# Two chained matrix products on one core: narrower plain block and wider product blocks, block sums in PSUM, shared weight slots, a first weight load in two pieces

## The chip, the cores and the metric

The kernel runs on one core of one Trainium2 chip. The metric is the device time of one execution in microseconds; less is better. The runs shown are the median of three executions of the kernel before.

## The reference

`x` has 8 batch elements of 256 rows and 1024 columns. For each element an adapter matrix (1024 x 1024, picked by an id) is applied, and a layer with low-rank experts is applied to the result. Everything is float32.

```
y    = x[b] @ weight[ids[b]].T                     # 256 x 1024
base = y @ base_W.T + base_b                       # 1024 outputs
p    = softmax(y @ router_W.T + router_b)          # 15 logits
w    = per expert (8): sum of the 8 largest p that map to it
h    = y @ A.T                                     # 8 experts x 16 ranks = 128 columns
out  = x + base + ((h * w) @ B) * 2
```

## The kernel before, in words

**Splits.** Almost every float32 operand is split into a high part in the type fp32r (a copy on ACT) and a low part (original minus high part, on DVE). A product is then high times high, plus high times low, plus low times high: three matmuls in fp32r. In stage 1 the moving operand carries high and low part of x side by side, so there the three are one of 512 and one of 256 columns.

**Work per element.** The eight elements run one after the other; element 0 and element 1 are written out, elements 2 to 6 are a loop, element 7 is written out again. An element has two stages on TensorE (PE).

- Stage 1 makes y transposed, in 8 chunks of 128 outputs. A chunk is `stage1_chunk`: 8 pairs of a 512-column matmul (L783) and a 256-column one (L785), into one of two PSUM banks `y_ps`. Before a chunk, PE waits for the chunk's weight split (`w_lo`) and for the running sum `y_sum` of the chunk two before it, which frees its bank. The first two chunks of element 0 skip the split and run as plain float32 matmuls (`stage1_float32`, L796; each shows as two records), which wait for `w0_in` and `x0_in`.
- Stage 2 multiplies y by the base matrix. `plain` (L807 to L809) does A, the router and the first NP = 288 base columns in one pass of 128 + 16 + 288 = 432 columns, 48 matmuls an element. The other 736 base columns are two halves N1 and N2 of NH = 368. With the two halves of the contraction and the two row tiles of y this is a 2 x 2 by 2 x 2 block product; it is done with 7 block products (`product`, L819 to L821, 12 matmuls each) in place of 8, on sums of blocks: S1, S2, S3 of y blocks and T1 to T4 of base blocks. Element 0 uses the plain 8 products, since the sums of base blocks are not there yet. `transposes` (L839) turns the gated h; `lora_b` (L833 to L835) multiplies it by B, into the same PSUM banks.

**Around PE.** Per chunk, ACT copies one half of the bank out and casts weights (`w_hi`, L362) and y (`y_hi`, L358); DVE adds the other half (`y_sum`, L503), and makes `w_lo` (L485) and `y_lo` (L507). After each pair of chunks DVE makes the y block sums (L513, L514, L516, `sums`) in SBUF, ACT casts them (`sums_hi`) and DVE makes `s_lo` (L520). S4 needs y and S2 and comes from `fourth`. DVE also does the router's softmax and top-8 on small tiles, adds the bias to the residual tile `res` and adds each finished PSUM bank into `res`. In element 1 DVE makes T3 and T4 (L679, L682) between chunks, and the low parts of T1 to T4 (L686, L690, L695) behind the last chunk.

**Order.** Each engine's order is written out by hand in its block, and semaphores tie the engines. Weights have 4 slots: SP loads the chunk for slot c when PE has finished the chunk that used it, ACT and DVE split it three chunks ahead. SP's queue carries all loads but the first two halves of x (ACT's queue), and all stores but those of element 0 (POOL's queue). Chunks 4 to 7 of element 0 are loaded early, into memory that later holds other tiles (`early_raw`).

```python
def stage1_chunk(b, c):
    s = c % W_SLOTS
    pe.wait_ge(w_lo_done, split(b, c))
    pe.wait_ge(y_sum_done, OC * b + c - 1)
```

## Time and profile before

| | |
|---|---|
| median of 3 runs | 406.89 us (406.59 to 407.56) |
| the profiled execution | 407.73 us, its span 405.9 us |
| granted TensorE clock, mean | 1.00 of 2.4 GHz |
| PE busy (matmuls) | 98% of the span |
| weight loads (PEld) busy | 92% |
| DVE busy | 73% |
| ACT busy | 38% |
| DMA | 64.7 MB, mean 159 GB/s |

The span runs from the first to the last instruction; the execution's own time is 1.8 us more. PE is one row of matmuls and PEld one row of the loads of their stationary operand, which overlap the matmuls. The recorded length of a matmul holds its way through the array, so matmuls overlap in the records; what one costs in a dense stretch is the time from its start to the next one's start.

### The profile page before, as it was taken

To read this page: it belongs to the slowest core of one execution; us is meant where nothing else is said; L and a number is where in the kernel's file an instruction comes from. 1 tells how busy PE (TensorE), PEld (TensorE's weight loads), DVE (VectorE), ACT (ScalarE), POOL (GpSimd) and SP (SyncE) were. 2 spreads that over 40 slices of the span, in tenths; PEclk is the share of its full clock that TensorE was granted. 3 is DMA by queue.
4 is the path that set the end of the run, shared out by engine and by line. 5 is a ranking of instruction groups with operands and counts; after the bars stand their busy time and mean duration, and the time that the engine had idled before them with its cause. 6 is when DMAs were issued, how large, how long until landed. Compare 5 with 4: busy or idle time off the path is not lost.

```text
span 405.9 us, 6358 instructions
## 1 busy us (share of the span) xinstructions
PE 398.8 (98%) x2278; PEld 371.6 (92%) x2278; DVE 295.8 (73%) x575; ACT 154.9 (38%) x236; POOL 2.0 (0%) x10
## 2 busy tenths in 40 slices
PE   7999999899999999999999999999999999999997
PEld 7889998789988999889998899989998899988996
DVE  2778985999959973788638885499754997467743
ACT  3675425563046220562216630165203643045200
POOL 0000000000000000000000000000000000000000
DMA  8999016660067602585025830468105770154002
GB/s 299 399 400 393 20 42 216 256 214 0 2 242 278 204 0 96 174 297 157 0 111 199 303 110 0 157 218 291 57 7 200 245 272 0 52 200 164 1 2 103
DMA packets 24878, 64.73 MB, mean 159 GB/s; under 512 B 2466, under 2 KB 11042, under 8 KB 24866
## 3 DMA queue, kind: packets, MB, share of 16 engines
q1 hardware_dynamic: 24290, 62.48, 42.9%
q10 hardware_dynamic: 288, 1.05, 0.8%
q0 software_dynamic: 288, 1.05, 0.6%
q8 instruction: 7, 0.11, 0.1%
q14 instruction: 5, 0.04, 0.0%
HBM read 56.18 MB, written 8.39 MB: 159 GB/s over the span
## 4 chain that ended last, share of the span: by engine, by line
PE 91%; DVE 4%; DMA 2%; ACT 1%; issue 1%; SPq 0%
PE y_ps L783 26%; PE y_ps L785 13%; PE pl_ps L807 6%; PE pl_ps L809 6%; PE pl_ps L808 6%; PE x_ps L821 5%; PE x_ps L820 5%; PE x_ps L819 5%; PE z_ps L819 3%; PE z_ps L820 3%; PE z_ps L821 3%; DMA w_raw<-in_wT 2%; PE y_ps L796 2%; PE w_ps L819 1%; PE w_ps L821 1%; PE w_ps L820 1%
## 5 line engine op out<-in xcount | busy, mean ns | idle before, releaser
L783 PE MATMUL y_ps<-x_split,w_hi 128*128 128x512 f32 x496 | 172.9, 394 | 1.2 <-DVE y_sum L503 1.2
L785 PE MATMUL y_ps<-x_split,w_lo 128*128 128x256 f32 x496 | 137.6, 277 | 0.0
L783 PEld LDWEIGHTS y_ps<-x_split,w_hi 128*128 128x128 f32 x496 | 93.0, 187 | 22.9 <-DVE w_lo L485 0.9
L785 PEld LDWEIGHTS y_ps<-x_split,w_lo 128*128 128x128 f32 x496 | 93.2, 188 | 0.0
L485 DVE TENSOR_TENSOR w_lo<-w_raw,w_hi 128x1024 fp32r<-128x1024 f32 x58 | 70.8, 1224 | 12.6 <-ACT w_hi L362 10.3
L354 ACT COPY y_sum<-y_ps 128x256 f32<-128x256 f32 x62 | 23.1, 373 | 122.2 <-PE y_ps L785 122.2
L362 ACT CAST w_hi<-w_raw 128x1024 fp32r<-128x1024 f32 x58 | 60.7, 1050 | 10.3 <-DMA w_raw<-in_wT 10.1
L503 DVE TENSOR_TENSOR y_sum<-y_ps,y_sum 128x256 f32<-128x256 f32 x62 | 26.1, 421 | 29.8 <-ACT y_sum L354 29.5
L807 PE MATMUL pl_ps<-pl_hi,y_hi 128*128 128x432 f32 x128 | 45.7, 357 | 0.2 <-DVE y_lo L507 0.2
L809 PE MATMUL pl_ps<-pl_hi,y_lo 128*128 128x432 f32 x128 | 45.8, 358 | 0.0
L808 PE MATMUL pl_ps<-pl_lo,y_hi 128*128 128x432 f32 x128 | 45.7, 357 | 0.0
L591 DVE TENSOR_TENSOR res<-x_ps,res 128x368 f32<-128x368 f32 x29 | 15.7, 540 | 30.0 <-PE x_ps L821 17.9
L358 ACT CAST y_hi<-y_sum 128x512 fp32r<-128x512 f32 x32 | 19.9, 621 | 21.1 <-DVE y_sum L503 20.6
L507 DVE TENSOR_TENSOR y_lo<-y_sum,y_hi 128x512 fp32r<-128x512 f32 x32 | 22.2, 692 | 5.5 <-ACT y_hi L358 2.7
L807 PEld LDWEIGHTS pl_ps<-pl_hi,y_hi 128*128 128x128 f32 x128 | 24.0, 188 | 1.8 <-DVE y_lo L507 0.6
L808 PEld LDWEIGHTS pl_ps<-pl_lo,y_hi 128*128 128x128 f32 x128 | 24.0, 187 | 1.0
L809 PEld LDWEIGHTS pl_ps<-pl_hi,y_lo 128*128 128x128 f32 x128 | 24.0, 188 | 0.9
L821 PE MATMUL x_ps<-st_hi,y_lo 128*128 128x368 f32 x64 | 21.1, 329 | 0.0
L819 PE MATMUL x_ps<-st_hi,y_hi 128*128 128x368 f32 x64 | 21.1, 329 | 0.0
L820 PE MATMUL x_ps<-st_lo,y_hi 128*128 128x368 f32 x64 | 21.0, 329 | 0.0
L588 DVE TENSOR_TENSOR res<-res,bias 128x1024 f32<-128x1024 f32 x16 | 18.8, 1218 | 0.0
L820 PE MATMUL x_ps<-st_lo,s_hi 128*128 128x368 f32 x56 | 18.5, 330 | 0.0
(140 smaller groups left out, 600.3 us busy)
## 6 DMA issues: line engine op xcount, KB each, us to landing
w_raw<-in_wT SPq DMA_DIRECT2D x60, 512.0 KB, 3.3
res<-in_x SPq DMA_DIRECT2D x16, 512.0 KB, 4.6
x_raw<-in_xT SPq DMA_DIRECT2D x14, 512.0 KB, 5.9
out<-res SPq DMA_DIRECT2D x13, 512.0 KB, 2.6
early_raw<-in_wT SPq DMA_DIRECT2D x4, 512.0 KB, 8.7
hi_raw<-in_base_t SPq DMA_DIRECT2D x4, 368.0 KB, 9.9
st_raw<-in_base_t SPq DMA_DIRECT2D x4, 368.0 KB, 10.1
pl_raw<-in_base_t SPq DMA_DIRECT2D x2, 576.0 KB, 12.1
```

What stands on the lines that cost most here:

```text
L354: nc.scalar.copy(y_sum[:, ORDER[c], :], y_ps[:, c % 2, T:2 * T]).then_inc(y_part_done, 1)
L362: nc.scalar.copy(w_hi[:, c % W_SLOTS, :, :], w_raw[:, c % W_SLOTS, :, :]).then_inc(w_hi_done, 1)
L485: nc.vector.tensor_tensor(w_lo[:, s, :, :], w_raw[:, s, :, :], w_hi[:, s, :, :], ALU.subtract).then_inc(w_lo_done, 1)
L503: nc.vector.tensor_tensor(y_sum[:, o, :], y_ps[:, c % 2, 0:T], y_sum[:, o, :], ALU.add).then_inc(y_sum_done, 1)
L783: nc.tensor.matmul(y_ps[:, c % 2, :], w_hi[:, s, k, :], x_split[:, k, :, :].rearrange("p s t -> p (s t)"), start=(k == 0), stop=False)
L785: mm = nc.tensor.matmul(y_ps[:, c % 2, 0:T], w_lo[:, s, k, :], x_split[:, k, 0, :], start=False, stop=(k == KC - 1))
L807: nc.tensor.matmul(dst, hi, pl_hi[:, k, :], start=(c == 0), stop=False)
L808: nc.tensor.matmul(dst, hi, pl_lo[:, k, :], start=False, stop=False)
L809: mm = nc.tensor.matmul(dst, lo, pl_hi[:, k, :], start=False, stop=(c == KC - 1))
L819: nc.tensor.matmul(dst, hi(j), st_hi[:, j, block_of, :], start=begins and j == 0, stop=False, skip_group_check=not begins)
L820: nc.tensor.matmul(dst, hi(j), st_lo[:, j, block_of, :], start=False, stop=False, skip_group_check=not begins)
L821: mm = nc.tensor.matmul(dst, lo(j), st_hi[:, j, block_of, :], start=False, stop=(j == KH - 1), skip_group_check=not begins)
```

## The change

NP goes from 288 to 32, and so NH from 368 to 496, the `plain` pass from 432 to 176 columns. The memory for the wider blocks comes from the y sums: DVE writes S1, S2, S3 into the three PSUM banks `z_ps`, `w_ps`, `v_ps` (now one tensor `s_ps`), and their splits `s_hi`, `s_lo` lie over weight slots 2 and 3. So the sums are split once an element, behind the last chunk (`sums_hi`, `sums_lo` of 1536 elements), and chunks 2 and 3 of the next element are loaded only when `w_ps_done` says that the last product from the sums is through. Weights are split two chunks ahead, and that split now stands in front of the running sum of the chunk. `add_bias` is in two parts, one before the last running sums and one behind them; `add_plain` is one addition for both tiles. `plain` does most of its contraction for both row tiles first and the last pair of chunks at the end. The block splits are one instruction for each block (1984 elements). In element 0 the order of products is new: B00 for both tiles first, each added into a part of `res` that the same bank is then used for again (`p1_done`, `p1_added`), then B10, T1, B11. In element 1 the T sums and splits are spread over the chunks and stage 2. The first weight chunk comes in two loads of 256 KB, each with a semaphore.

```diff
-    NP = 288
+    NP = 32
...
+        s_hi = sb("s_hi", [P, 3, KH, P], F32R, over=at_w + 2 * 4 * KC * P)
+        s_lo = sb("s_lo", [P, 3, KH, P], F32R, over=at_w + (W_SLOTS + 2) * 4 * KC * P)
...
+        s_ps = bank("s_ps", [P, 3, 512])
+        z_ps, w_ps, v_ps = (s_ps[:, i, :] for i in range(3))
...
             def element(b, last=False):
...
-                    if c + W_SLOTS < OC or not last:
+                    if c + W_SLOTS < OC or (not last and c < W_SLOTS + 2):
                         sp.wait_ge(y_ps_done, OC * b + c + 1)
                         load_w(this if c + W_SLOTS < OC else nxt, (c + W_SLOTS) % OC)
...
                 if not last:
+                    sp.wait_ge(y_ps_done, OC * b + OC)
                     load_x(b + 1)
+                    sp.wait_ge(w_ps_done, b + 1)
+                    for c in (2, 3):
+                        load_w(nxt, c)
...
-            sp.dma_start(w_raw[:, 0, :, :], wT[bass.ds(id0, 1), 0].rearrange("a p k o -> (a p) k o")).then_inc(w0_in, 16)
+            for j in range(PIECES):
+                k = slice(j * KP, (j + 1) * KP)
+                sp.dma_start(w_raw[:, 0, k, :], wT[bass.ds(id0, 1), 0, :, k, :].rearrange("a p k o -> (a p) k o")).then_inc(w0_in[j], 16)
...
-            def sums_lo(b, j):
-                dve.wait_ge(s_hi_done, KH * (b - 1) + j + 1)
-                nc.vector.tensor_tensor(s_lo[:, j, :, :], s_raw[:, j, :, :], s_hi[:, j, :, :], ALU.subtract).then_inc(s_lo_done, 1)
+            def sums_lo(b):
+                dve.wait_ge(s_hi_done, b)
+                nc.vector.tensor_tensor(s_lo[:, :, :, :], s_ps[:, :, :].rearrange("p s (j t) -> p s j t", t=P), s_hi[:, :, :, :],
+                                        ALU.subtract).then_inc(s_lo_done, 1)
...
                 for c in range(OC):
+                    if not last or c + 2 < OC:
+                        adapter_lo(b, c + 2)
                     make_y_sum(b, c)
                     if c % 2:
                         sums(b, c // 2)
                         dve.wait_ge(s_done, KH * (b - 1) + c // 2 + 1)
                         make_y_lo(b, c // 2)
-                    if not last or c + 3 < OC:
-                        adapter_lo(b, c + 3)
-                    if c % 2:
-                        sums_lo(b, c // 2)
...
+            block_lo(1, B00, r00)
+            block_sum_1()
+            block_lo(2, B10, r10)
             masks()
-            block_sums_1_2()
             routing_logits(0)
+            dve.wait_ge(res_in[0], 16)
+            dve.wait_ge(p1_done, 1)
+            add(0, N2, w_ps[:, 0:NH]).then_inc(p1_added, 1)
+            t1_lo()
+            dve.wait_ge(res_in[1], 16)
+            dve.wait_ge(p1_done, 2)
+            add(1, N2, x_ps[:, 0:NH]).then_inc(p1_added, 1)
             routing_gates(0)
...
-            def plain(b, t, first=False):
-                dst = pl_ps[:, t, 0:PL]
-                for c, k in enumerate(PLAIN_ORDER):
...
+            def plain(b, first=False):
+                for t, part in ((1, 0), (0, 0), (1, 1), (0, 1)):
+                    for k in PLAIN_ORDER[:KC - 2] if part == 0 else PLAIN_ORDER[KC - 2:]:
...
-                product(z_ps, y_block(0, 0), T1, wait_blocks=1)
-                product(z_ps, y_block(1, 0), B11, begins=False, wait_blocks=2)
-                product(x_ps, y_block(0, 1), T1)
-                product(x_ps, y_block(1, 1), B11, begins=False).then_inc(b01_free, 1)
...
+                product(w_ps, y_block(0, 0), B00).then_inc(p1_done, 1)
+                product(x_ps, y_block(0, 1), B00).then_inc(p1_done, 1)
+                pe.wait_ge(blocks_lo_done, 2)
+                pe.wait_ge(p1_added, 1)
+                product(w_ps, y_block(1, 0), B10, begins=False)
+                pe.wait_ge(p1_added, 2)
+                product(x_ps, y_block(1, 1), B10, begins=False)
+                pe.wait_ge(t_lo_done, 1)
+                product(z_ps, y_block(0, 0), T1)
```

The first place where the order moves is DVE's in stage 2 of element 0, on which PE's new waits rest. `st_lo` and `st_raw`, `hi_raw` are the low parts and the raw blocks of the base matrix, `res<-s_ps` is the addition of the first B00 product. Before:

```order
L507 TENSOR_TENSOR y_lo<-y_sum,y_hi 128x2x256
L656 TENSOR_TENSOR st_lo<-hi_raw,st_hi 128x2x2x368
L653 TENSOR_TENSOR st_lo<-st_raw,st_hi 128x2x736
L656 TENSOR_TENSOR st_lo<-hi_raw,st_hi 128x2x2x368
L653 TENSOR_TENSOR st_lo<-st_raw,st_hi 128x2x736
L661 CAST map_f<-map_i 128x15
L664 TENSOR_SCALAR expert_mask<-map_f 128x15 x8
L672 TENSOR_TENSOR hi_raw<-hi_raw 128x4x368
L674 TENSOR_TENSOR st_raw<-st_raw,hi_raw 128x4x368
L540 TENSOR_TENSOR logits<-pl_ps,router_bias 128x30
```

And now:

```order
L515 TENSOR_TENSOR y_lo<-y_sum,y_hi 128x2x256
L668 TENSOR_TENSOR st_lo<-hi_raw,st_hi 128x4x496
L684 TENSOR_TENSOR hi_raw<-hi_raw 128x4x496
L668 TENSOR_TENSOR st_lo<-st_raw,st_hi 128x4x496
L672 CAST map_f<-map_i 128x15
L675 TENSOR_SCALAR expert_mask<-map_f 128x15 x8
L550 TENSOR_TENSOR logits<-pl_ps,router_bias 128x30
```

followed, behind the rest of the logits' work, by

```order
L600 TENSOR_TENSOR res<-s_ps,res 128x496
L702 TENSOR_TENSOR st_lo<-hi_raw,st_hi 128x4x496
L600 TENSOR_TENSOR res<-x_ps,res 128x496
```

The two additions of half-finished output (L600) are new; they stand behind three instructions on 1984 elements, the masks and the logits.

The second place is DVE's order in element 1, chunks 1 and 2, where PE waited before. Before:

```order
L503 TENSOR_TENSOR y_sum<-y_ps,y_sum 128x256
L513 TENSOR_TENSOR s_raw<-y_sum 128x128
L514 TENSOR_TENSOR s_raw<-y_sum 128x128
L516 TENSOR_TENSOR s_raw<-s_raw,y_sum 128x128
L507 TENSOR_TENSOR y_lo<-y_sum,y_hi 128x2x256
L485 TENSOR_TENSOR w_lo<-w_raw,w_hi 128x1024
L520 TENSOR_TENSOR s_lo<-s_raw,s_hi 128x384
L503 TENSOR_TENSOR y_sum<-y_ps,y_sum 128x256
L485 TENSOR_TENSOR w_lo<-w_raw,w_hi 128x1024
L679 TENSOR_TENSOR st_raw<-st_raw,hi_raw 128x4x368
L503 TENSOR_TENSOR y_sum<-y_ps,y_sum 128x256
```

And now:

```order
L493 TENSOR_TENSOR w_lo<-w_raw,w_hi 128x1024
L511 TENSOR_TENSOR y_sum<-y_ps,y_sum 128x256
L522 TENSOR_TENSOR s_ps<-y_sum 128x128
L523 TENSOR_TENSOR s_ps<-y_sum 128x128
L525 TENSOR_TENSOR s_ps<-s_ps,y_sum 128x128
L515 TENSOR_TENSOR y_lo<-y_sum,y_hi 128x2x256
L493 TENSOR_TENSOR w_lo<-w_raw,w_hi 128x1024
L511 TENSOR_TENSOR y_sum<-y_ps,y_sum 128x256
```

The split of the sums is gone from between the chunks, the weight split stands in front of the running sum, and the T sum that stood in front of chunk 3's running sum (L679) has moved to chunk 0.

## Rows read from the trace of the kernel before

**Rows 1.** The page, busy time of each engine and its share.

```profile
PE 398.8 (98%) x2278; PEld 371.6 (92%) x2278; DVE 295.8 (73%) x575; ACT 154.9 (38%) x236; POOL 2.0 (0%) x10
```

**Rows 2.** By stretch: its length, busy PE, PEld, DVE, ACT, POOL, then granted clock, DMA.

```profile
133.22:142.60 9.38, 9.38 (x51) 9.01 (x49) 8.14 (x14) 2.98 (x5) 0.00 (x0) 1.00 0.56 171
142.60:159.67 17.07, 17.07 (x106) 17.04 (x104) 10.34 (x30) 2.49 (x4) 0.00 (x0) 1.00 0.08 31
65.16:83.58 18.42, 17.21 (x98) 14.60 (x97) 16.03 (x29) 10.89 (x18) 0.00 (x0) 1.00 0.64 232
83.58:111.03 27.45, 26.95 (x154) 25.93 (x153) 25.90 (x47) 9.46 (x11) 0.00 (x0) 1.00 0.18 59
```

**Rows 3.** Timeline, the first matmuls of element 3's stage 1.

```profile
159.67 0.40 PE L783 MATMUL y_ps<-x_split,w_hi 128*128 128x512 f32 x1
159.90 0.28 PE L785 MATMUL y_ps<-x_split,w_lo 128*128 128x256 f32 x1
160.02 0.39 PE L783 MATMUL y_ps<-x_split,w_hi 128*128 128x512 f32 x1
```

**Rows 4.** Timeline, PE behind a wait in element 1's `plain`.

```profile
87.43 0.19 PEld L807 LDWEIGHTS pl_ps<-pl_hi,y_hi 128*128 128x128 f32 x1 [0.55 <-DVE y_lo L507]
...
87.54 0.19 PEld L808 LDWEIGHTS pl_ps<-pl_lo,y_hi 128*128 128x128 f32 x1
...
87.74 0.36 PE L808 MATMUL pl_ps<-pl_lo,y_hi 128*128 128x432 f32 x1
```

**Rows 5.** Timeline of element 2's stage 2: start, length, engine, line.

```profile
142.60 0.33 PE L819 MATMUL x_ps<-st_hi,y_hi 128*128 128x368 f32 x1
...
144.60 0.33 PE L819 MATMUL z_ps<-st_hi,s_hi 128*128 128x368 f32 x1
...
156.38 0.29 PE L833 MATMUL pl_ps<-b_hi,hwt_hi 128*128 128x288 f32 x1
156.51 0.29 PE L834 MATMUL pl_ps<-b_lo,hwt_hi 128*128 128x288 f32 x1
```

**Rows 6.** Timeline, weight loads behind the two 128-column transposes, element 1.

```profile
99.57 0.19 PEld L819 LDWEIGHTS w_ps<-st_hi,y_hi 128*128 128x128 f32 x1
...
99.68 0.19 PEld L820 LDWEIGHTS w_ps<-st_lo,y_hi 128*128 128x128 f32 x1
```

**Rows 7.** Timeline of DVE in element 0's stage 2.

```profile
33.44 1.68 DVE L656 TENSOR_TENSOR st_lo<-hi_raw,st_hi 128x1472 fp32r<-128x1472 f32 x1
35.04 1.69 DVE L653 TENSOR_TENSOR st_lo<-st_raw,st_hi 128x1472 fp32r<-128x1472 f32 x1
...
39.85 0.17 DVE L661 CAST map_f<-map_i 128x15 f32<-128x15 int32 x1
...
40.78 1.69 DVE L672 TENSOR_TENSOR hi_raw<-hi_raw 128x1472 f32<-128x1472 f32 x1
...
44.12 0.18 DVE L540 TENSOR_TENSOR logits<-pl_ps,router_bias 128x30 f32<-128x30 f32 x1
...
45.20 0.18 DVE L556 TENSOR_REDUCE row_sum<-prob 128x2 f32<-128x30 f32 x1
```

**Rows 8.** Timeline of PE, the first matmul behind element 0's stage 1.

```profile
31.11 0.36 PE L807 MATMUL pl_ps<-pl_hi,y_hi 128*128 128x432 f32 x1
```

**Rows 9.** DMA issues: count, KB each, median us from issue to landing.

```profile
w_raw<-in_wT SPq DMA_DIRECT2D x60, 512.0 KB, 3.3
```

**Rows 10.** Timeline, the change from float32 chunks to split chunks in element 0.

```profile
11.35 1.04 ACT L362 CAST w_hi<-w_raw 128x1024 fp32r<-128x1024 f32 x1 [0.23 <-DMA w_raw<-in_wT]
...
13.57 0.42 DVE L733 COPY y_sum<-y_ps 128x256 f32<-128x256 f32 x1
...
14.47 0.19 PEld L785 LDWEIGHTS y_ps<-x_split,w_lo 128*128 128x128 f32 x1
```

**Rows 11.** Timeline, the end of the program.

```profile
403.00 0.54 DVE L591 TENSOR_TENSOR res<-x_ps,res 128x368 f32<-128x368 f32 x1 [2.02 <-PE x_ps L835]
```

**Rows 12.** The tile `w_raw` to 40 us: count, shortest, median, longest ns, first and last start.

```profile
L796 PE MATMUL y_ps<-x_raw,w_raw x32: 379/379/483, 7.5 to 14.2; 128*128 128x256 f32 x32
```

More of the change, by code:

```diff
@@ L109, in adaln_ffn_kernel @@
         res = sb("res", [P, NT, D])
-        early_raw = [sb(f"early_raw{i}", [P, KC, P], over=at) for i, at in
-                     enumerate((at_s + 4 * KC * T, at_bias, at_res, at_res + 4 * D))]
+        x0_raw = sb("x0_raw", [P, KC, T], over=at_res)
+        early_raw = [sb(f"early_raw{i}", [P, KC, P], over=at_st + i * 4 * 7 * NH) for i in range(OC - W_SLOTS)]
         at_hwt = spot[0]
@@ L157, in adaln_ffn_kernel @@
         pl_in = [sem(f"pl_in{h}") for h in range(2)]
-        st_in = [sem(f"st_in{j}") for j in range(KH)]
+        upper_in = sem("upper_in")
+        lower_in = sem("lower_in")
         b_in = sem("b_in")
@@ L323, in _ @@
             for j in range(KH):
-                load_blocks(j)
+                load_upper(j)
+            for j in range(KH):
+                load_lower(j)
             for src, dst in ((expert_map, map_i), (router_b, router_bias)):
@@ L458, in _ @@
                 if c == 6:
-                    blocks_hi(0, 0)
-            blocks_hi(0, 1)
-            blocks_hi(1, 0)
-            blocks_hi(1, 1)
+                    act.wait_ge(upper_in, 16 * KH)
+                    act.wait_ge(w_lo_done, split(0, OC - 1))
+                    block_hi(B00, hi_raw[:, :, T4, :])
+            act.wait_ge(lower_in, 16 * KH)
+            block_hi(B10, st_raw[:, :, T4, :])
+            act.wait_ge(t_done, 1)
+            nc.scalar.copy(st_hi[:, :, T1, :], hi_raw[:, :, T2, :]).then_inc(t1_hi_done, 1)
+            block_hi(B11, st_raw[:, :, T3, :])
             exponential(0)
-            make_x_hi(1)
             act.wait_ge(b_in, 16)
@@ L609, in stage2 @@
                 add(1, N2, z_ps[:, 0:NH]).then_inc(z_added, 1)
+                if second:
+                    t3_lo()
+                else:
+                    fourth(b)
                 dve.wait_ge(x_ps_done, x_adds(b, 2))
@@ L614, in stage2 @@
                     fourth(b)
-                    fourth_lo(b)
-                if not last:
+                fourth_lo(b)
+                if not last and not second:
                     make_x_lo(b + 1)
@@ L621, in stage2 @@
                 if second:
+                    t4_lo()
+                    make_x_lo(b + 1)
                     dve.wait_ge(x_added, x_adds(b, 3))
-                    add_bias(b)
+                    for t in range(NT):
+                        add_bias(b, t)
                     dve.wait_ge(res_biased, 2 * b + 2)
@@ L703, in element @@
                         make_y_lo(b, c // 2)
-                    if not last or c + 3 < OC:
-                        adapter_lo(b, c + 3)
-                    if c % 2:
-                        sums_lo(b, c // 2)
-                    if isinstance(b, int) and b == 1 and c == 2:
-                        block_sum_3()
-                    if isinstance(b, int) and b == 1 and c == 6:
-                        block_sum_4()
-                if isinstance(b, int) and b == 1:
-                    t1_lo()
-                    t34_lo()
-                    t2_lo()
-                    routing_logits(b)
-                else:
-                    add_bias(b)
-                    fourth(b)
-                    fourth_lo(b)
-                    routing_logits(b)
+                    if second and c == 0:
+                        block_sum_4()
+                    if second and c == 4:
+                        t2_lo()
+                    if not second and c == 6:
+                        add_bias(b, 0)
+                if second:
+                    block_sum_3()
+                else:
+                    add_bias(b, 1)
+                sums_lo(b)
+                routing_logits(b)
                 stage2(b, last)
@@ L852, in first_stage2 @@
+                product(x_ps, y_block(0, 1), B00).then_inc(p1_done, 1)
[6 more added lines that the diff above has]
+                product(z_ps, y_block(0, 0), T1)
                 pe.wait_ge(hw_done, 1)
                 transposes()
-                product(w_ps, y_block(0, 0), B00)
@@ L855, in first_stage2 @@
-                product(w_ps, y_block(1, 0), B10, begins=False)
+                pe.wait_ge(blocks_lo_done, 3)
+                product(z_ps, y_block(1, 0), B11, begins=False)
                 pe.wait_ge(b_lo_done, 1)
                 pe.wait_ge(hwt_lo_done, 1)
+                lora_b(0, w_ps[:, 0:NH], N1).then_inc(w_ps_done, 1)
                 lora_b(0, z_ps[:, 0:NH], N2).then_inc(z_ps_done, 1)
-                lora_b(1, x_ps[:, 0:NH], N2).then_inc(x_ps_done, 1)
-                lora_b(0, w_ps[:, 0:NH], N1).then_inc(w_ps_done, 1)
+                lora_b(1, x_ps[:, 0:NH], N1).then_inc(x_ps_done, 1)
@@ L861, in first_stage2 @@
                 for t in range(NT):
                     lora_b(t, pl_ps[:, t, AR:PL], PLAIN).then_inc(pl_ps_done, 1)
-                product(v_ps, y_block(0, 1), B00)
-                product(v_ps, y_block(1, 1), B10, begins=False)
-                lora_b(1, v_ps[:, 0:NH], N1).then_inc(v_ps_done, 1)
+                product(v_ps, y_block(0, 1), T1)
+                product(v_ps, y_block(1, 1), B11, begins=False)
+                lora_b(1, v_ps[:, 0:NH], N2).then_inc(v_ps_done, 1)
             def stage2(b):
-                pe.wait_ge(pl_added, 2 * b)
```

211 lines of the change are left out of this document (102 added, 109 removed).

## Prediction, made blind

> **What bounds the kernel now.** The page comes first: matmuls are busy for 98% of the span, weight loads for 92%, DVE for 73% [rows 1]. PE is the bound, so I price PE's rows from start to start, and ask only where PE waits. In element 2 nothing waits: the busy time of both stretches equals their length, 9.38 us for `plain` and 17.07 us for the rest [rows 2]. The granted clock there is 1.00, the 2.4 GHz level. Element 1 is the exception. Its stage 2 takes 27.45 us against 9.38 + 17.07 = 26.45 us in element 2, and its chunks 2 to 7 take 18.42 us where six chunks of eight pairs at 0.347 us are 16.64 us [rows 2, 3]. That is 2.8 us of waiting on DVE; one of the waits, 0.55 us for `y_lo`, is shown [rows 4].
>
> What a matmul costs, start to start: 432 columns 9.38 / 48 = 0.195 us [rows 2]; 368 columns 2.00 / 12 = 0.167 us [rows 5]; 512 columns 0.23 and 256 columns 0.12 us [rows 3]; 288 columns 0.13 us [rows 5]. All lie on one line, columns / 2.4 GHz + 13 ns, within 2 ns. So 496 columns cost 0.220 us, between two known widths.
>
> **The narrow pass** is the term that decides, and no row shows a moving operand under 256 columns in fp32r. The line gives (176 + 32) / 2.4 = 0.087 us. But each matmul needs a weight load of its own, and the load for the next one starts when the present one starts. Behind a wait, where PE is empty, the first load starts at 87.43 and the second, which can begin once the first matmul streams, at 87.54; the second matmul starts at 87.74, one 0.195 us matmul later [rows 4]. Behind the transposes two loads are again 0.11 us apart [rows 6]. So a load takes 0.109 us before its matmul can stream. At 256 columns and more it is hidden (0.12 us); at 176 it is not. The bounds are 0.087 us (load hidden) and 0.120 us (the narrowest fp32r row, 256 columns). I take 0.109, the row that shows the load alone. The six 32-column matmuls of `lora_b` cost 0.109 each too, against 0.13 before.
>
> On this the Trainium skill, "TensorE: Matmul & The Clock Gate", section "Back-to-back issue gap", says columns / 2.4 + 2.5 ns for an isolated stream, with a floor near 25 ns. That is an estimate of 76 ns for 176 columns and would put the total near 396 us; the traced widths contradict its constant (13 ns, not 2.5). The same page's section "LDWEIGHTS (loading the stationary operand)" gives 128 / 1.2 = 107 ns for the load, which the 0.109 us row agrees with.
>
> **The change, part by part.**
> 1. *Elements 1 to 7, each.* `plain` 48 x (0.109 - 0.195) = -4.13 us. Seven products 84 x (0.220 - 0.167) = +4.45. `lora_b` on N1 and N2 12 x 0.053 = +0.64; its plain columns 6 x (0.109 - 0.132) = -0.14. Sum +0.82, times seven +5.7 us.
> 2. *Element 0* has eight products: -4.13 + 96 x 0.053 + 0.64 - 0.14 = +1.5 us.
> 3. *New waits in element 0.* PE reaches the second use of `w_ps` after `plain` 5.2 and two B00 products 5.3, 10.5 us behind stage 1. It waits there for DVE's first partial addition. DVE is done with `y_lo` at 33.44, 2.3 us behind stage 1, which ends at 31.11 [rows 7, 8]. A 1472-element instruction holds it 1.60 us (33.44 to 35.04), 1.09 ns an element, so 1984 take 2.15. Three of them, the masks 0.93 (39.85 to 40.78), the logits 1.08 (44.12 to 45.20) [rows 7], and an addition of 496 (0.5) end at 11.3. With the 0.2 us that PE takes behind a DVE result (DVE 13.57 + 0.42, seen below) that is a stall of 1.0 us; the second addition, behind one more 2.15 us split, costs 0.1. **+1.1 us.** T1's split, the gates and B11's split are 2 us or more ahead of PE.
> 4. *Element 1.* Out of each pair of chunks goes the split of the sums (0.5 us), and a 1.7 us T sum no longer stands in front of chunk 3's running sum. By the same lengths, laid out in DVE's new order, every running sum is 0.5 to 1 us early but that of chunk 5, level with PE. In stage 2 the 5.35 us of T3 and T4 splits lie in front of nothing PE needs. Of 2.8 us I leave 0.4: **-2.4 us.** If this is not so, what is late is `w_lo` of chunk 7, at one DVE instruction, 2 us.
> 5. *Sums split at once.* From the end of stage 1: y sum, y cast and `y_lo` 2.3, bias 1.1, then 1536 elements 1.7 us: 5.1 us. PE needs them after `plain` and one product, at 5.2 + 2.6 = 7.8. Hidden by 2.7 us; with a 0.087 us pass by 1.7. `fourth` (three instructions of 512 elements, 1.7 us) now stands in front of the second x addition, which needs the S2 product's end at 13.2 in any case; DVE has it by 14.0, PE asks behind the transposes and one more product, at 16.1. Nothing.
> 6. *Weight slots 2 and 3.* Their loads start 5.3 us before the element's end (two `lora_b` blocks of 0.66, the narrow one, the T4 product and its `lora_b`); a load lands in 3.3 us at the median [rows 9], a cast and a split of 1024 take 1.04 [rows 10] and 1.1. Chunk 2 needs them 5.5 us into the next element: 5 us to spare. Behind the waiting SP stand only the stores, which need later results. Without that cover, each late load would stop DVE's running sum too, since the split now stands in front of it. Nothing.
> 7. *First weight chunk in two loads.* PE starts at 7.45 us, waiting for it; half of it lands perhaps 0.9 us sooner. But PE then meets the next wait: chunk 2 of element 0 needs `y_sum` of chunk 0, which DVE does behind two weight splits that hang on the fourth weight load (landed at 11.35): it ends at 13.99, and PE's first split chunk streams from 14.47 [rows 10]. With 0.2 us behind DVE it can stream from 14.2. **-0.25 us** (between 0 and -0.3). The extra issue on SP delays nothing that PE waits for. The last addition and store are 128 columns wider, +0.13 and a little: the addition of 368 took 0.54 [rows 11]: **+0.15 us.**
>
> Sum: 5.7 + 1.5 + 1.1 - 2.4 - 0.25 + 0.15 = **+5.8 us**. The profiled execution took 407.73 us, 0.8 above the median of 406.89; so it would be 413.5, and the median **412.7 us**.
>
> **Rivals.**
> - *The load is hidden after all* (0.087 and 0.027 us): 48 x 0.022 + 6 x 0.082 = 1.55 us less in each of eight elements, 12.4; `plain` is then 1.1 shorter in element 0, which adds 1.1 to the first stall: 412.7 - 12.4 + 1.1 = **401.4 us, faster**. For it: the two columns-only fits are exact wherever they can be read, and a load's start may be free to move ahead when the matmul is short. Against it: [rows 4, 6]. It decides from the width at which (columns + 32) / 2.4 is below 0.109 us, 230 columns.
> - *The 256-column cost is the floor*, 0.120 us: 54 x 0.011 x 8 = +4.8: **417.5 us.** For it: that row is the narrowest one there is, and the 13 ns may come on top of the load. Against it: the 0.11 us of [rows 4, 6].
> - *Narrow fp32r goes at float32's pace.* The plain float32 chunks run 32 records in 6.8 us, 0.213 us each and two a matmul, so 1.67 ns a column [rows 12]; 176 columns then cost 0.293: 48 x 0.184 x 8 = +71: **483 us.** Nothing in the trace speaks for it but that no narrow pass is there.
> - *DVE is late in element 1 as before* (part 4 gives nothing): 415.1 us. DVE has 73% of the span filled [rows 1] and the T sums are a third longer each.
>
> **How the numbers follow.** The forecast's case, 410.5 to 415.5 us, has 0.62, of which the late DVE is the upper end; the 256-column floor 0.12; the hidden load 0.16; float32's pace 0.06; anything near no change (a load hidden in part, with every wait gone) 0.04. The range of 400.5 to 418.0 us leaves out the third rival and the tails, 0.1 in all. A measurement here can tell 0.2%, 0.8 us, from no change. Faster by more 0.17, within it 0.04, slower 0.79.
>
> **What would show it.** `plain` of a middle element at 5.2 us in place of 9.38, its 176-column rows 0.109 us apart and weight loads back to back with them; 7 products at 2.64 us each; an element 0.8 us longer. A wait of 1 us on DVE in front of the third product of element 0, none over 0.3 us in element 1. `plain` near 4.2 us, 5.8 us or 14 us would each name its rival. Waits of PE on `w_lo` of chunks 2 and 3 would prove part 6 wrong.

## The result, and the profile of the changed kernel

The changed kernel takes **419.29 us** (median of 4, 418.96 to 419.58), the kernel before beside it 407.23 us: a ratio of 1.030, 95% interval 1.028 to 1.0316. It is slower, as forecast, but by 12.1 us where the forecast said 5.8, and outside the range. Profile against profile it is 417.8 - 405.9 = 11.9 us.

The page's first part answers to [rows 1]. PE is still the bound; the weight loads have lost 13 us of busy time for the same number of them, since more of their 0.19 us records now overlap (busy time counts an overlap once): a first sign that loads stand close together somewhere.

```profile
PE 409.9 (98%) x2278; PEld 358.1 (86%) x2278; DVE 301.2 (72%) x548; ACT 154.0 (37%) x215; POOL 2.0 (0%) x10
```

The stretches that answer to [rows 2]: length, busy PE, PEld, DVE, ACT, POOL, clock, DMA share and GB/s. In order: `plain` and the rest of stage 2 of element 3, stage 1 and the whole stage 2 of element 1, `plain` of element 2.

```profile
186.68:192.01 5.33, 5.33 (x50) 5.33 (x49) 5.17 (x8) 2.44 (x3) 0.00 (x0) 1.00 0.60 194
192.01:214.46 22.45, 22.45 (x106) 18.94 (x105) 13.12 (x33) 4.05 (x6) 0.00 (x0) 1.00 0.18 63
63.00:86.39 23.39, 22.68 (x130) 19.40 (x129) 19.77 (x29) 12.47 (x18) 0.83 (x2) 1.00 0.62 226
86.39:114.14 27.75, 27.75 (x154) 24.25 (x153) 25.11 (x44) 8.45 (x10) 0.00 (x0) 1.00 0.22 76
136.34:142.04 5.70, 5.57 (x51) 5.41 (x49) 5.54 (x10) 2.63 (x4) 0.00 (x0) 1.00 0.57 184
```

In `plain` of element 3, PEld is busy for 5.33 of 5.33 us: the loads stand back to back, 5.33 / 48 = 0.111 us each, and set the pace. In the blocks they have room (18.94 of 22.45 us). The granted clock is 1.00 in both.

The timeline of PE where element 3 goes from stage 1 to `plain` and from there to the first product. Starts in the first column.

```profile
186.68 0.24 PE L838 MATMUL pl_ps<-pl_hi,y_hi 128*128 128x176 f32 x1
186.76 0.28 PE L839 MATMUL pl_ps<-pl_lo,y_hi 128*128 128x176 f32 x1
186.87 0.28 PE L840 MATMUL pl_ps<-pl_hi,y_lo 128*128 128x176 f32 x1
186.98 0.27 PE L838 MATMUL pl_ps<-pl_hi,y_hi 128*128 128x176 f32 x1
...
192.01 0.42 PE L849 MATMUL x_ps<-st_hi,y_hi 128*128 128x496 f32 x1
192.26 0.38 PE L850 MATMUL x_ps<-st_lo,y_hi 128*128 128x496 f32 x1
192.49 0.39 PE L851 MATMUL x_ps<-st_hi,y_lo 128*128 128x496 f32 x1
```

Read the starts, not the lengths (which say 0.24 to 0.28 us for a narrow matmul). The first narrow step is 0.08 us, from then on it is 0.11. The same holds 23 us on for the 32-column matmuls of `lora_b`, which are 5.5 times narrower and cost the same:

```profile
210.56 0.26 PE L865 MATMUL pl_ps<-b_hi,hwt_lo 128*128 128x32 f32 x1
210.67 0.26 PE L863 MATMUL pl_ps<-b_hi,hwt_hi 128*128 128x32 f32 x1
```

**Where the 11.9 us are,** from the starts of the elements in both traces (59.62, 111.03, 159.67, ... 354.17 us before; 63.00, 114.14, 164.48, 214.46, ... 364.40 after), with the forecast's terms by stretch:

| stretch | before | after | change | forecast |
|---|---|---|---|---|
| start to `plain` of element 0 | 31.11 | 31.73 | +0.62 | -0.25 |
| stage 2 of element 0 | 28.51 | 31.27 | +2.76 | +2.6 |
| element 1 | 51.41 | 51.14 | -0.27 | -1.6 |
| element 2 | 48.64 | 50.34 | +1.70 | +0.8 |
| elements 3 to 6, each | 48.63 | 49.98 | +1.35 | +0.82 |
| element 7 and the end | 51.73 | 53.40 | +1.67 | +1.0 |

**Element 0.** The wait that the forecast placed in front of the third product is there. PE's rows, and DVE's: the first T-size split and the addition of the first product.

```profile
42.23 0.38 PE L851 MATMUL x_ps<-st_hi,y_lo 128*128 128x496 f32 x1
43.22 0.46 PE L849 MATMUL s_ps<-st_hi,y_hi 128*128 128x496 f32 x1 [0.60 <-DVE res L600]
```

```profile
34.06 2.22 DVE L668 TENSOR_TENSOR st_lo<-hi_raw,st_hi 128x1984 fp32r<-128x1984 f32 x1
...
42.41 0.67 DVE L600 TENSOR_TENSOR res<-s_ps,res 128x496 f32<-128x496 f32 x1
```

From 42.23 to 43.22 is 0.99 us where a matmul costs 0.22: a stall of 0.77 us, forecast 1.0. DVE's addition ends at 43.08, 11.35 us behind stage 1 (31.73), as forecast (11.3). It is PE that comes later than forecast, after 10.7 us in place of 10.5, because its own matmuls are dearer; and it starts 0.14 us behind DVE in place of 0.2.

**Element 1.** Of the 1.8 us of stage-1 waits before, 1.2 us are left. ACT's rows first, then DVE's, then the weight loads that show PE's waits.

```profile
72.19 1.86 ACT L430 CAST st_hi<-st_raw 128x1984 fp32r<-128x1984 f32 x1
73.95 1.04 ACT L376 CAST w_hi<-w_raw 128x1024 fp32r<-128x1024 f32 x1
```

```profile
75.02 1.23 DVE L493 TENSOR_TENSOR w_lo<-w_raw,w_hi 128x1024 fp32r<-128x1024 f32 x1 [1.40 <-ACT w_hi L376]
...
79.70 2.21 DVE L707 TENSOR_TENSOR st_lo<-st_raw,st_hi 128x1984 fp32r<-128x1984 f32 x1
81.83 1.22 DVE L493 TENSOR_TENSOR w_lo<-w_raw,w_hi 128x1024 fp32r<-128x1024 f32 x1
```

```profile
79.89 0.19 PEld L813 LDWEIGHTS y_ps<-x_split,w_hi 128*128 128x128 f32 x1 [0.41 <-DVE w_lo L493]
83.50 0.19 PEld L813 LDWEIGHTS y_ps<-x_split,w_hi 128*128 128x128 f32 x1 [0.89 <-DVE w_lo L493]
```

ACT's copy of T4's high half (72.19, 1.86 us) stands in front of the cast of weight chunk 5 (73.95), so DVE is idle for 1.40 us and does that split at 75.02; everything behind it is late by as much, and the split of T2 at 79.70 adds 2.2 us more in front of the next weight split. PE waits for `w_lo` in front of chunk 6 (0.3 us) and of chunk 7 (0.75 us).

**Element 2.** `plain` waits 0.37 us for `y_lo` (5.70 us in place of 5.33). The wait begins with a weight load that takes 4.97 us to land, issued at 125.58: ACT's cast behind it, at 130.57, waits 1.53 us for it, and DVE's split, which stands in front of the running sum, is idle for 1.29 us in turn. In `one_load` below the order is the same, that load lands in 3.20 us, and `plain` does not wait.

**The start.** The timeline: PE's plain float32 chunks, the third weight cast, the copy that frees PE's bank, and PE's first split chunk.

```profile
7.61 7.14 PE L825 MATMUL y_ps<-x_raw,w_raw 128*128 128x256 f32 x32 [1.43 <-DMA w_raw<-in_wT]
10.96 1.04 ACT L376 CAST w_hi<-w_raw 128x1024 fp32r<-128x1024 f32 x1 [4.02 <-DMA w_raw<-in_wT]
...
14.45 0.42 DVE L754 COPY y_sum<-y_ps 128x256 f32<-128x256 f32 x1
...
15.01 0.47 PE L813 MATMUL y_ps<-x_split,w_hi 128*128 128x512 f32 x1 [0.26 <-DVE y_sum L754]
```

In this pair of profiles PE starts no sooner for the load in two pieces (7.61, before 7.45), and what comes behind is later: the cast at 10.96 stood at 10.08 before, and PE's split chunks, at 14.28 before, start at 15.01. How far that is the edit's doing is asked below.

### The profile page after: what moved, and what is told of

Read it like the earlier page. It is cut to its first block, busy times and chain, and to the rows that moved or that the text cites. A ratio compares the mean times of both kernels' runs of the same rounds, so it can differ in the third digit from the quotient of the medians.

```text
span 417.8 us, 6304 instructions
## 1 busy us (share of the span) xinstructions
PE 409.9 (98%) x2278; PEld 358.1 (86%) x2278; DVE 301.2 (72%) x548; ACT 154.0 (37%) x215; POOL 2.0 (0%) x10
## 4 chain that ended last, share of the span: by engine, by line
PE 85%; DVE 6%; DMA 3%; ACT 3%; issue 1%; SPq 1%; DVEq 0%
PE y_ps L813 23%; PE y_ps L815 12%; PE x_ps L849 6%; PE x_ps L850 6%; PE x_ps L851 6%; PE s_ps L849 6%; PE s_ps L850 6%; PE s_ps L851 6%; DMA w_raw<-in_wT 3%; PE pl_ps L839 3%; PE pl_ps L838 3%; PE pl_ps L840 3%; DVE w_lo L493 2%; ACT w_hi L376 1%; PE s_ps L864 1%
## 5 line engine op out<-in xcount | busy, mean ns | idle before, releaser
L600 DVE TENSOR_TENSOR res<-x_ps,res 128x496 f32<-128x496 f32 x30 | 20.2, 674 | 41.5 <-PE x_ps L851 21.6
L839 PE MATMUL pl_ps<-pl_lo,y_hi 128*128 128x176 f32 x128 | 35.1, 274 | 0.0
L840 PE MATMUL pl_ps<-pl_hi,y_lo 128*128 128x176 f32 x128 | 35.1, 274 | 0.0
L838 PE MATMUL pl_ps<-pl_hi,y_hi 128*128 128x176 f32 x128 | 34.9, 273 | 0.1
L600 DVE TENSOR_TENSOR res<-s_ps,res 128x496 f32<-128x496 f32 x32 | 21.3, 674 | 17.2 <-PE s_ps L865 17.1
L849 PE MATMUL s_ps<-st_hi,y_hi 128*128 128x496 f32 x80 | 31.8, 397 | 0.6 <-DVE res L600 0.6
L850 PE MATMUL s_ps<-st_lo,y_hi 128*128 128x496 f32 x80 | 31.0, 387 | 0.0
L851 PE MATMUL s_ps<-st_hi,y_lo 128*128 128x496 f32 x80 | 30.9, 386 | 0.0
L849 PE MATMUL x_ps<-st_hi,y_hi 128*128 128x496 f32 x64 | 25.6, 399 | 0.0
L850 PE MATMUL x_ps<-st_lo,y_hi 128*128 128x496 f32 x64 | 24.7, 386 | 0.0
L851 PE MATMUL x_ps<-st_hi,y_lo 128*128 128x496 f32 x64 | 24.7, 386 | 0.0
```

What stands on the lines that cost most here:

```text
L600: return nc.vector.tensor_tensor(res[:, t, cols], ps, res[:, t, cols], ALU.add)
L838: nc.tensor.matmul(dst, hi, pl_hi[:, k, :], start=(k == 0), stop=False)
L839: nc.tensor.matmul(dst, hi, pl_lo[:, k, :], start=False, stop=False)
L840: mm = nc.tensor.matmul(dst, lo, pl_hi[:, k, :], start=False, stop=(k == KC - 1))
L849: nc.tensor.matmul(dst, hi(j), st_hi[:, j, block_of, :], start=begins and j == 0, stop=False, skip_group_check=not begins)
L850: nc.tensor.matmul(dst, hi(j), st_lo[:, j, block_of, :], start=False, stop=False, skip_group_check=not begins)
```

## The experiments

Eleven kernels ran, in three groups. Every ratio is against the kernel before, run beside its group (medians 407.73, 407.63 and 407.87 us). An interval behind a ratio is a 95% interval.

### The width alone: `np288_rest`

The changed kernel with the block widths of before; everything else of the change stays.

```diff
-    NP = 32
+    NP = 288
```

> The changed kernel with NP = 288 (NH = 368) again: the width undone, all the rest kept. Theory one, the widths make most of the loss: PE's rows go back to 0.195 us (432 columns) and 0.167 us (368 columns), so elements 2 to 7 are 1.35 us shorter each than in the changed kernel (48.6 us), element 0 some 2 to 2.9 us, element 1 more than 1.35; about 12 us less in all, 406 to 408 us. Rival, the new order, the sums in PSUM and the shared slots make it: the time stays above 411 us. Also told: a wait in element 0 on the partial additions shrinks, since plain is 4 us longer there.

Measured: 409.15 us, ratio 1.0035 (1.0022 to 1.0049). So of 12 us the width makes some 10.7 (419.29 against 409.15, ratio against ratio) and all the rest 1.4. The windows of element 3's stage 2, `plain` and the rest:

```profile
183.49:192.88 9.39, 9.39 (x51) 9.01 (x49) 5.48 (x8) 2.44 (x3) 0.00 (x0) 1.00 0.35 112
192.88:209.96 17.08, 17.08 (x105) 17.05 (x104) 12.13 (x32) 3.70 (x6) 0.00 (x0) 1.00 0.17 63
```

These are the 9.38 and 17.07 us of [rows 2]: sums in PSUM, shared slots and one split an element give and cost nothing in a middle element (48.66 us, before 48.63). Profile against profile the difference is 1.8 us: the start (`plain` of element 0 at 32.08, before 31.11) and element 2 (49.53, before 48.64), less 0.2 us in element 1. Element 1's gain is eaten by a wait of 0.8 us in stage 2 and by one late load: ACT waits for it (first line below), PE then waits in front of chunk 4 for the split behind it.

```profile
69.99 1.05 ACT L376 CAST w_hi<-w_raw 128x1024 fp32r<-128x1024 f32 x1 [1.90 <-DMA w_raw<-in_wT]
```

```profile
72.75 0.19 PEld L813 LDWEIGHTS y_ps<-x_split,w_hi 128*128 128x128 f32 x1 [1.25 <-DVE w_lo L493]
```

Element 2 is long for the same reason. PE waits in front of chunk 4 at 123.5 us for the split of weights that ACT got at 120.73, after 1.72 us of waiting. Their slot was free when PE had done chunk 0, at 114.56. But SP issues the last two stores of element 1 only at 113.50, 1.7 us into element 2 (before: 110.99, at its start), and the load behind them at 117.19: 2.6 us after the slot was free, in the kernel before 0.9 us (113.81 and 114.72).

### A pass above the floor: `np112_256cols`

```diff
-    NP = 32
+    NP = 112
```

> The changed kernel with NP = 112 (NH = 456), so that the plain pass has 256 columns. If the weight load sets a floor of 0.111 us under a narrow matmul, plain costs 0.120 us a matmul (5.8 us an element against 5.3), while each of 96 wide matmuls loses 40 columns, 0.017 us: 1.2 us less an element, about 410 us in all. If matmuls of 496 columns are also dearer than their columns say (0.2245 against 0.220 us measured), and 456 are not, another 0.4 us an element goes, 406 to 407 us. If narrow passes were not floored, 256 columns would cost 0.033 us more each than 176, and the time would not fall.

Measured: 410.56 us, 1.0067 (1.0042 to 1.0091). `plain` of 256 columns and the blocks of 456, element 5; and three starts of `plain`:

```profile
231.65:237.41 5.76, 5.76 (x50) 5.76 (x49) 5.40 (x8) 2.44 (x3) 0.00 (x0) 1.00 0.61 182
237.41:258.17 20.76, 20.76 (x106) 18.87 (x105) 12.64 (x32) 4.06 (x6) 0.00 (x0) 1.00 0.17 58
```

```profile
231.77 0.28 PE L839 MATMUL pl_ps<-pl_lo,y_hi 128*128 128x256 f32 x1
231.89 0.29 PE L840 MATMUL pl_ps<-pl_hi,y_lo 128*128 128x256 f32 x1
232.01 0.28 PE L838 MATMUL pl_ps<-pl_hi,y_hi 128*128 128x256 f32 x1
```

256 columns cost 0.120 us, 176 cost 0.111: 80 columns less, 33 ns by the line, buy 9 ns. The matmuls of 112 columns in this kernel's `lora_b` cost 0.111 us as well. Going from 176 to 256 columns takes 0.43 us more in `plain` and 22.45 - 20.76 = 1.69 us less in the rest: most of the loss lies in the last 80 columns. The 456-column matmuls take 2.48 / 12 = 0.207 us, 4 ns over the line. One thing was not expected: stage 1, which no width touches, is slower here. Its pairs are 0.35 us apart instead of the 0.347 of [rows 3], at granted clock 1.00:

```profile
215.40 0.40 PE L813 MATMUL y_ps<-x_split,w_hi 128*128 128x512 f32 x1
215.63 0.28 PE L815 MATMUL y_ps<-x_split,w_lo 128*128 128x256 f32 x1
215.75 0.40 PE L813 MATMUL y_ps<-x_split,w_hi 128*128 128x512 f32 x1
```

A chunk takes 2.82 us instead of 2.77, some 0.4 us an element; without it, by estimate, this kernel would be near 408 us. Other kernels fall into the same rhythm for a part of their time (`after_again` in element 0, `np288_rest` in element 2 from the wait at 123.5 us on). Some of the changes come at a wait of PE, but in element 2 of this kernel the rhythm changes at 122.3 us without one. What picks it stays open.

### The other direction: `before_np368`

The kernel before with a wider pass, 512 columns, and blocks of 328.

```diff
-    NP = 288
+    NP = 368
```

> The kernel before with NP = 368 (NH = 328), the width moved the other way: plain has 512 columns, the blocks 328. Theory: a base column costs 48 matmuls an element in plain and half of 84 + 12, that is 48, in the blocks, so above the weight load's floor the width is neutral: no change within 0.5 us. If instead narrower blocks were worth something by themselves (the 4.5 ns above the line at 496 columns), it is faster by more than 1 us; if wider blocks paid, slower by more.

Measured: 408.45 us, 1.0015 (0.9993 to 1.0036): no difference that the runs can tell. Windows of element 3's stage 2:

```profile
181.96:192.88 10.92, 10.92 (x50) 9.02 (x49) 9.51 (x14) 2.98 (x6) 0.00 (x0) 1.00 0.48 155
192.88:208.58 15.70, 15.70 (x105) 15.68 (x104) 9.88 (x29) 2.49 (x4) 0.00 (x0) 1.00 0.07 29
```

An element takes 48.81 us, 0.18 more than before. This is the arithmetic that the forecast had in its terms and did not draw: each base column is streamed through 48 matmuls of `plain` and 6 of `lora_b`, 54 in all, and in the blocks through (84 + 12) / 2 = 48. 80 columns moved are 80 x 6 / 2.4 GHz = 0.20 us. **Above the floor the width is nearly neutral**: even 200 columns moved free of charge would give 0.5 us an element.

### Width or layout: `products_368_of_496`

The changed kernel whose products use 368 of their 496 columns, in every matmul but the first of a bank.

```diff
-                    nc.tensor.matmul(dst, hi(j), st_lo[:, j, block_of, :], start=False, stop=False, skip_group_check=not begins)
+                    nc.tensor.matmul(dst, hi(j), st_lo[:, j, block_of, 0:368], start=False, stop=False, skip_group_check=True)
```

> The changed kernel with each product computed on 368 of its 496 columns only, apart from the first matmul of a fresh bank; memory, strides and order stay. It leaves out the other columns' sums. It asks why a 496-column matmul takes 0.2245 us where columns / 2.4 + 13 ns gives 0.220. If it is the width, a row of 12 takes 2.01 us (0.1675 each); if it is the layout (the stride between rows of the wider blocks), each stays 4 ns over, 2.06 us.

One execution: 388.17 us, for less work. A product that opens no bank takes 2.01 us for its twelve matmuls (187.83 to 189.84, granted clock 1.00), as 368 columns did before (2.00); the one 496-column matmul that opens a bank is seen beside the others:

```profile
185.75 0.39 PE L850 MATMUL s_ps<-st_hi,s_hi 128*128 128x496 f32 x1
185.98 0.33 PE L852 MATMUL s_ps<-st_lo,s_hi 128*128 128x368 f32 x1
186.14 0.33 PE L853 MATMUL s_ps<-st_hi,s_lo 128*128 128x368 f32 x1
```

So the new layout (sums in other memory, wider strides) costs nothing; what the 496-column matmuls take over the line, 0.2245 us against 0.220, comes with their width.

### The first load in one piece: `one_load`

```diff
-            for j in range(PIECES):
-                k = slice(j * KP, (j + 1) * KP)
-                sp.dma_start(w_raw[:, 0, k, :], wT[bass.ds(id0, 1), 0, :, k, :].rearrange("a p k o -> (a p) k o")).then_inc(w0_in[j], 16)
+            sp.dma_start(w_raw[:, 0, :, :], wT[bass.ds(id0, 1), 0].rearrange("a p k o -> (a p) k o")).then_inc(w0_in[0], 16)
```

> The changed kernel with the first weight chunk in one load of 512 KB again. Theory: two loads of 2 KB packets delay every load behind them, and the fourth weight load sets when the first split chunk can run, so undoing it starts that chunk about 0.7 us sooner: 418.6 us. Rival, the delay has another cause (the later issues on SP, the float32 pass itself): no change, or slower by the half chunk's lead.

Measured: 418.92 us, 1.0272 (1.0251 to 1.0293). The time is within the noise of the changed kernel's, the profile is not: the third weight cast and the first split chunk are back where they were before (10.08 and 14.28 us).

```profile
10.16 1.04 ACT L374 CAST w_hi<-w_raw 128x1024 fp32r<-128x1024 f32 x1 [3.27 <-DMA w_raw<-in_wT]
...
14.29 0.58 PE L811 MATMUL y_ps<-x_split,w_hi 128*128 128x512 f32 x1
```

That is 0.7 us in this pair of profiles. It is not shown to be the edit's doing. `np288_one_load_t4` and `one_load_t4`, with one load too, have the third cast at 10.98 and 10.68 us and the first split chunk at 15.02 and 15.03; the six profiles of kernels with two loads have the chunk at 14.77 to 15.14, each time behind a wait for `y_sum`. Nor is it shown that two pieces bring no lead: PE starts its float32 chunks at 7.01 to 7.61 us in those six and at 7.45 to 8.66 in the seven with one load.

Three kernels that start with the code of the kernel before have the first split chunk at 15.31, 16.82 and 17.14 us. The first of them has its load landed a microsecond late. The two others have that and a slower TensorE as well: PE stood idle for 2.30 and 2.23 us in front of the float32 chunks, the granted clock was 0.50 (the level of 1.2 GHz) for the next 3 us, and a record there took 0.427 us in place of 0.216. From `before_tsums_early`, the row and the windows of the slow part and of the whole:

```profile
8.50 8.67 PE L796 MATMUL y_ps<-x_raw,w_raw 128*128 128x256 f32 x32 [2.30 <-DMA w_raw<-in_wT]
...
8.50:11.60 3.10, 3.10 (x7) 2.52 (x8) 0.00 (x0) 0.57 (x1) 0.00 (x0) 0.50 1.03 416
8.50:16.82 8.32, 8.32 (x32) 7.10 (x33) 3.92 (x4) 4.18 (x4) 0.00 (x0) 0.82 1.02 415
```

From the first float32 matmul to the first split one it is 8.32 and 8.48 us there, 6.82 us at clock 1.00.

### ACT's copy of T4 behind the sums: `t4_late`

```diff
-                    if isinstance(b, int) and b == 1 and c == 2:
-                        act.wait_ge(t_done, 3)
-                        nc.scalar.copy(st_hi[:, :, T4, :], st_raw[:, :, T4, :]).then_inc(t4_hi_done, 1)
...
                 sums_hi(b)
+                if isinstance(b, int) and b == 1:
+                    act.wait_ge(t_done, 3)
+                    nc.scalar.copy(st_hi[:, :, T4, :], st_raw[:, :, T4, :]).then_inc(t4_hi_done, 1)
```

> The changed kernel with ACT's copy of T4 in element 1 behind the sums' copy, in place of in chunk 2. Theory: that copy delays the weight cast of chunk 5 by 1.9 us, and since the split stands in front of the running sum, it delays the sums of chunks 3 to 5; PE's 1.2 us of waits in element 1 go, 418.1 us. Rival: DVE is simply full there, with a T2 split of 2.2 us in chunk 4, and at least 0.8 us of waits stay.

Measured: 417.77 us, 1.0253 (1.023 to 1.0277). Element 1 takes 49.95 us, as long as a middle element: with that one copy moved, all its waits are gone. The split of chunk 5's weights follows right behind the running sum; in the changed kernel, whose element 1 starts 0.26 us later, it came at 75.02 us behind 1.40 us of idling:

```profile
72.94 0.42 DVE L511 TENSOR_TENSOR y_sum<-y_ps,y_sum 128x256 f32<-128x256 f32 x1
73.27 1.22 DVE L493 TENSOR_TENSOR w_lo<-w_raw,w_hi 128x1024 fp32r<-128x1024 f32 x1
```

### Both repairs: `one_load_t4`, beside `after_again`

> The changed kernel with both small repairs together: the first weight chunk in one load again, and ACT's copy of the sum block T4 in the second element behind the high halves of its first sums. If the two repairs act on separate places and add up, it shows 0.5 to 0.9 us (start) and 0.9 to 1.3 us (stage-1 waits of the second element) less than the changed kernel of the same call: about 417.3 us, and element 2 without a wait in its plain matmuls. If what the one saves is given back at the next wait, it stands at 418 us or more. Either way it stays above 1.02 of the kernel before, since the width of 496 columns is untouched.

> The changed kernel as it is, for comparison with the two repairs on the same chip: 419.3 us, 1.03 of the kernel before; elements from the third on of 49.98 us each, narrow matmuls of 0.111 us, matmuls of 496 columns of 0.2245 us.

Measured side by side: 418.91 us, 1.0273 (1.024 to 1.0307), against 419.19 us, 1.0265 (1.0236 to 1.0293). No gain that the runs can tell. Element 1 does go from 51.19 to 50.50 us, and the wait in `plain` of element 2 (0.8 us in `after_again`, 0.37 in the first profile) is gone. But its start is late in this profile (15.03 us), and a weight load of element 1 lands late. DVE waits 0.70 us for the cast behind it, and 0.5 us of waits are there again in stage 1:

```profile
73.63 1.05 ACT L374 CAST w_hi<-w_raw 128x1024 fp32r<-128x1024 f32 x1 [0.95 <-DMA w_raw<-in_wT]
```

The expected sum of the two gains was not shown. What is: neither repair, nor both, touches the 2.5% of the width.

### Both repairs at the old width: `np288_one_load_t4`

The edits of `one_load` and `t4_late`, with NP = 288.

> The changed kernel with NP = 288, the first weight chunk in one load and the T4 copy late. NP = 288 alone was 1.4 us above the kernel before. Theory: 0.7 us of that is the two loads, and the T4 copy gives the rest of element 1 back only in part, since its wait there hangs on a late weight load: 408.0 to 408.5 us. Rival, sums in PSUM and split once are worth something once the waits are gone: at or under 407 us.

Measured: 409.12 us, 1.0037 (1.002 to 1.0054), no better than `np288_rest`. Element 1 keeps a wait of 0.81 us in front of chunk 4 and one of 0.79 us in front of the B11 product, element 2 one of 0.25, in front of chunk 4 again; elements 3 to 6 take 48.66 us. The hope that the new staging is worth something once its waits are gone is not borne out: the two repairs did not take them away, and where there are none an element is no shorter than before.

### Only what helped in element 1: `before_tsums_early`

The kernel before, with its T3 sum at the head of element 1 and its T4 sum behind the first running sum, in place of behind chunks 2 and 6.

```diff
             def element(b, last=False):
+                if isinstance(b, int) and b == 1:
+                    block_sum_3()
                 for c in range(OC):
                     make_y_sum(b, c)
+                    if isinstance(b, int) and b == 1 and c == 0:
+                        block_sum_4()
...
-                    if isinstance(b, int) and b == 1 and c == 2:
-                        block_sum_3()
-                    if isinstance(b, int) and b == 1 and c == 6:
-                        block_sum_4()
```

> The kernel before, unchanged but for DVE's two T sums of element 1, which move from chunks 2 and 6 to in front of chunk 0 and behind its running sum, where DVE sat idle for 2.6 us. Theory: they are what made PE wait in chunks 4 to 7 (1.8 us) and, by the late y_lo and the late fourth sum, twice in stage 2 (0.9 us): 2.7 us go, about 404.9 us beside 407.5 of the kernel before. Rival: DVE is full in element 1 in any order, and the waits come back in other chunks: less than 1 us is won.

Measured: 406.57 us against 407.63, ratio 0.9971 (0.9952 to 0.999). Element 1, stage 1 and stage 2:

```profile
62.16:84.35 22.19, 22.19 (x129) 19.40 (x129) 19.89 (x32) 12.35 (x20) 0.53 (x1) 1.00 0.71 257
84.35:111.32 26.97, 26.66 (x154) 25.99 (x153) 24.48 (x46) 9.46 (x11) 0.00 (x0) 1.00 0.19 63
```

Stage 1 is dense. Element 1 takes 49.16 us where it took 51.41 in the first profile, 2.25 us less; the medians are only 1.06 us apart, and where the rest goes is not shown. What is left in the element is a wait of 0.47 us in front of the B11 product, for the low half of S4 (of which the row shows 0.30):

```profile
104.45 0.41 PE L819 MATMUL z_ps<-st_hi,y_hi 128*128 128x368 f32 x1 [0.30 <-DVE y_lo L532]
```

### One step further: `tsums_v2`

The edit of `before_tsums_early`, and on top of it:

```diff
                 add(1, N2, z_ps[:, 0:NH]).then_inc(z_added, 1)
+                if second:
+                    fourth(b)
                 dve.wait_ge(x_ps_done, x_adds(b, 2))
                 add(0, N2, x_ps[:, 0:NH]).then_inc(x_added, 1)
                 make_hwt_lo(b)
                 if second:
-                    fourth(b)
                     fourth_lo(b)
```

> The kernel before with the sums of its weight blocks moved ahead in the second element, as in before_tsums_early, and with the combination of the fourth sums of that element (DVE) started directly behind the first add of the z products instead of behind the add after it and the routing split. If the 0.47 us that the sum-block product of the second element still waited for a low half is DVE's order alone, the wait goes and element 1 takes 48.7 us instead of 49.2, and the kernel about 406.1 us (0.996 of before). If another input of the product is as late (ACT's copy of the high half), the wait stays near 0.4 us and the time at 0.997. If DVE's later add holds a bank, a new wait stands at the next product.

Measured: 406.04 us against 407.87, ratio 0.9954 (0.9935 to 0.9974), the lowest median of all kernels here that do the full work. Its stage 2 of element 1 is dense now:

```profile
85.25:111.90 26.65, 26.65 (x155) 26.01 (x153) 25.15 (x46) 9.67 (x12) 0.00 (x0) 1.00 0.20 68
```

The wait went, so it was DVE's order. But element 1 takes 49.12 us, not the 48.7 expected: 0.3 us of a new wait stand in front of chunk 6 of its stage 1, for which the trace names no releaser. So against `before_tsums_early` the gain is not shown; against the kernel before it is.

## Why the prediction was right or wrong

- **What bounds the kernel.** Right. PE has 98% in both, and the whole difference is in PE's own starts.
- **The narrow pass, 0.109 us: right** (0.111), and the rivals that would have made it 0.087, 0.120 or 0.293 are out. 32, 112 and 176 columns cost the same, with the loads back to back, so it is the load that paces them. The Trainium skill, "TensorE: Matmul & The Clock Gate", section "LDWEIGHTS (loading the stationary operand)", gives 128 / 1.2, an estimate of 107 ns, for a load of 128 columns, which these rows bear out within 4 ns. Its section "Back-to-back issue gap" says that sustained pairs of load and matmul at 128 columns come about 81 ns apart; here 32 and 176 columns in fp32r both stand at 0.111 us, and the trace decides. These 2 ns are 54 x 8 x 0.002 = 0.9 us of the miss.
- **Part 1, the products: mis-sized.** The step that failed is "496 columns cost 0.220 us, between two known widths". They cost 0.2245 us (rows of twelve 2.68 to 2.70 us): there are 7 x 96 + 108 = 780 of them, and 780 x 0.0045 = 3.5 us, the largest share of the miss. 456 columns are over the line by 4 ns as well; 512 are not (10.92 / 48 = 0.2275 us in `before_np368`, line 0.226). The forecast's "within 2 ns" was not shown for the widest rows: [rows 3] give 0.23 us for 512 columns, and only the pair with 256 fits the line. `products_368_of_496` shows that the layout is no part of it; why the width has this cost is open.
- **Parts 2 and 3, element 0: right in kind, and close by luck.** The sum is right within 0.2 us because two errors meet: the matmuls are 0.6 us dearer than forecast (108 x 0.0045 and 54 x 0.002), and the stalls are 0.77 us in place of 1.1, since PE comes to them later.
- **Part 4, element 1: wrong in size.** -0.27 us against -1.6, 1.3 us short, of which 0.5 belong to part 1. The step laid out DVE's new order by its lengths and came out level or early at every running sum; it did not lay out ACT's. There the copy of T4's high half, 1.86 us, stands in front of a weight cast, and `t4_late` takes all of the element's stage-1 waits away by moving it. DVE's 2.2 us split of T2 stands in the same chain. Where the forecast said it would show if it was wrong, `w_lo` of chunk 7, there the larger wait is (0.75 us).
- **Part 5, sums split at once: right**, no wait for them in any element.
- **Part 6, shared slots: right for chunks 2 and 3, wrong for what it left out.** No wait of PE from element 3 on, and none for chunks 2 and 3. The 0.37 us in element 2 come from a late weight load, which stops DVE's running sum through the split in front of it; the forecast had named this way and gave it nothing. And behind SP's stores stands the load of chunk 4 too: at the old width its delay costs PE 0.6 us of waiting in element 2.
- **Part 7, the first load in two: no gain, size not shown.** Said -0.25, came +0.6 in the pair of profiles; the same start code differs by more from profile to profile. By the ranges over all thirteen, the lead of the first half may well be there (7.01 to 7.61 us against 7.45 to 8.66), but the split chunks wait for `y_sum` and start no sooner, the limit that the forecast named. The ratios of `one_load` and `after_again`, 1.0272 and 1.0265, tell no difference.

The miss, 6.1 us between the profiles, is then 3.5 us from the 496-column matmuls, 0.9 us from narrow ones, 1.2 us of waits in elements 1 and 2, 0.9 us at the start and 0.1 at the end, less 0.3 us of stall in element 0; together 6.3, with 0.2 of rounding. The range was too narrow above: its upper end held either the 256-column floor or the late DVE, but no error in a width that 780 matmuls have.

## What to carry to other kernels

When work moves between a wide and a narrow stream of matmuls, first count on both sides how many matmuls stream each column: here it was 54 against 48, so the best possible gain was small before any floor counted. Then find the width at which the load of the stationary operand paces the stream (here 0.111 us, by estimate some 235 columns on the line) and stop above it: 512 and 256 columns are within 0.7% of 432, and 176 columns are 3% off. And when a hand-written order is checked for lateness, lay out every engine in the chain, ACT and SP's queue as well as DVE.
